# Both tiles' long products first, and their diagonal blocks behind them, at eleven of 32 places of a fused attention and mixture-of-experts kernel

## What is computed

```python
q = q * cos + _rotate_half(q) * sin
k = k * cos + _rotate_half(k) * sin
attn = jnp.einsum('bhqd,bhkd->bhqk', q, k) * SCALE
diff = jnp.where(diff > 0, 0.0, diff)          # pos[key] - pos[query]
attn = attn + (diff[None, :, :] * slopes[:, None, None] * MAX_BIAS)[None]
w = jax.nn.softmax(attn, axis=-1)
out = jnp.einsum('bhqk,bhkd->bhqd', w, v)
```

## Time and profile before

| | |
|---|---|
| median of 3 runs | 1626.6 us (1621.5 to 1634.37) |
| span of the profiled execution | 1580.1 us |
| own time of the profiled execution | not recorded apart; the median is 46.5 us above its span |
| TensorE busy | 1439.4 us, 91% |
| VectorE busy | 1180.2 us, 75% |
| ScalarE busy | 1020.6 us, 65% |
| GpSimd busy | 720.8 us, 46% |
| mean granted TensorE clock | 0.955 |
| first and last score product | 28.1 and 1380.4 us |

### The profile page before, as it was taken

One profiled execution on the slowest core, in us unless ns is written; L12 is line 12 of the kernel. 1 busy time (PEld: TensorE's weight loads), 2 busy tenths in 40 slices (PEclk: granted clock), 3 DMA queues, 4 the chain that ended last, 5 costly groups with the idle time before them and its releaser, 6 DMA issues.

```text
span 1580.1 us, 33006 instructions
## 1 busy us (share of the span) xinstructions
PE 1439.4 (91%) x11110; PEld 785.8 (50%) x11110; DVE 1180.2 (75%) x2631; ACT 1020.6 (65%) x1742; POOL 720.8 (46%) x655
## 2 busy tenths in 40 slices
PE   8988999999999989899999999998999899998937
PEld 4433444444444435455555544454455555664625
DVE  7675787888787897766776778877877677736875
ACT  1365766676767656777777676766677676776242
POOL 3233353736455434552534354543647443437550
PEclk8699999999999999999999999999999999999969
DMA  7435344333343424455545434354577576697451
GB/s 208 131 93 177 101 132 118 118 104 120 112 138 113 127 87 134 160 169 155 184 152 167 158 113 129 111 159 135 173 233 227 182 228 205 215 290 223 139 167 41
DMA packets 176390, 242.00 MB, mean 153 GB/s; under 512 B 58024, under 2 KB 94975, under 8 KB 176223
## 3 DMA queue, kind: packets, MB, share of 16 engines
q1 hardware_dynamic: 145786, 181.18, 38.0%
q0 software_dynamic: 10752, 29.37, 5.9%
q10 hardware_dynamic: 19684, 29.33, 5.4%
HBM read 152.53 MB, written 91.44 MB: 154 GB/s over the span
## 4 chain that ended last, share of the span: by engine, by line
PE 60%; DVE 17%; DMA 6%; SPq 5%; issue 5%; POOL 4%; ACT 2%; ACTq 0%; POOLq 0%; DVEq 0%
PE pS L660 17%; PE pV L702 11%; PE pG L726 6%; DVE negm L951 6%; PE pG L735 4%; PE pG L829 3%; PE pG L837 3%; PE pG L748 3%; PE pS L666 3%; PE pG L821 2%; DMA d_rec<-scr 1%; POOL d_x L1611 1%; PE pG L797 1%; SPq L503 1%; PE pG L851 1%
## 5 line engine op out<-in xcount | busy, mean ns | idle before, releaser
L951 DVE TENSOR_REDUCE negm<-pS 128x1 f32<-128x512 f32 x1024 | 657.9, 682 | 261.8 <-PE pS L666 256.6
L1389 ACT ACTIVATE ee<-pT,slp 128x512 f32<-128x512 f32 x1024 | 648.8, 684 | 224.0 <-PE pT L687 222.0
L660 PE MATMUL pS<-ka,qa 62*128 62x512 f32 x1024 | 477.1, 502 | 72.1 <-DVE negm L951 63.7
L681 PE MATMUL pT<-qa,ka 64*128 64x512 f32 x1024 | 472.0, 496 | 0.2 <-ACT ee L1389 0.2
L660 PEld LDWEIGHTS pS<-ka,qa 62*128 62x128 f32 x1024 | 195.6, 191 | 337.9 <-issue 323.6
L702 PE MATMUL pV<-ee,vv 128*32 128x512 f32 (+1 forms) x2048 | 284.0, 627 | 0.0
L666 PE MATMUL pS<-mAB,tri 64*128 64x64 bf16 x2048 | 241.5, 199 | 0.0
L687 PE MATMUL pT<-mAB,tri 64*128 64x64 bf16 x2048 | 237.6, 197 | 0.0
L1576 POOL TENSOR_TENSOR raw<-raw,rope 128x512 f32<-128x512 f32 x61 | 78.4, 1285 | 273.2 <-DVE sh L986 273.0
L681 PEld LDWEIGHTS pT<-qa,ka 64*128 64x128 f32 x1024 | 192.9, 188 | 3.9 <-issue 3.1
L666 PEld LDWEIGHTS pS<-mAB,tri 64*128 64x128 bf16 x2048 | 118.6, 98 | 139.4 <-issue 110.6
(11 more groups left out here) (198 smaller groups left out, 2181.2 us busy)
## 6 DMA issues: line engine op xcount, KB each, us to landing
d_part<-parts SPq DMA_DIRECT2D x63, 512.0 KB, 2.8
qa<-d_part SPq DMA_DIRECT2D x378, 64.0 KB
wb<-in_wb SPq DMA_DIRECT2D x77, 256.5 KB
xg<-d_x SPq DMA_DIRECT2D x77, 256.0 KB, 2.9
d_y<-yb ACTq DMA_DIRECT2D x77, 256.0 KB, 3.3
ka<-d_part SPq DMA_DIRECT2D x128, 128.0 KB
xT<-in_xT SPq DMA_DIRECT2D x16, 512.0 KB, 4.2
ka<-d_part SPq DMA_DIRECT2D x128, 64.0 KB
```

The lines of the kernel that those rows point to most:

```text
L660: e.matmul(pS[:, k, :], qa[g % 4][r, i, t * 128:t * 128 + 128].bitcast(F32R), ka[g % 4][r, i, :].bitcast(F32R), start=True, stop=False)
L681: e.matmul(pT[:, k, :], ka[g % 4][r, i, kt * 128:kt * 128 + 128].bitcast(F32R), qa[g % 4][r, i, :].bitcast(F32R), start=True, stop=False)
L951: e.tensor_reduce(negm[:, g % 2, j, t + k:t + k + 1], pS[:, k, :], AX, ALU.max, negate=True).then_inc(s_max, 1)
L1389: e.activation(ee[:, k, d % 7, :], pT[:, k, :], ACT.Exp, scale=slp[:, 6, h:h + 1]).then_inc(s_exp, 1)
```

## The change

A tuple names eleven places, and at these `pair(s)` no longer writes the blocks of tile 0 behind the long products of tile 0. It writes both long products of tile 0, both of tile 1, and then the blocks of tile 0 and of tile 1. At the other 21 places the order stays. No instruction is added or taken away, and the other engines' programs are the same.

```diff
 APART = tuple(range(32))
+LATE_BLOCKS = (0, 9, 10, 11, 22, 26, 27, 28, 29, 30, 31)
...
-            apart = s % 32 in APART
             for k in range(2):
                 if 0 <= s < NC:
                     score_rows(s, k)
                 if 0 <= d < NC:
                     turned_rows(d, k)
-                for kk in ((k,) if apart else (0, 1) if k == 1 else ()):
+                for kk in (() if s % 32 in LATE_BLOCKS and k == 0 else (0, 1) if s % 32 in LATE_BLOCKS else (k,)):
                     for a in range(2):
                         if 0 <= s < NC:
                             score_block(s, kk, a)
                         if 0 <= d < NC:
                             turned_block(d, kk, a)
```

## The result

The change made the kernel slightly slower in the comparison that belongs to the prediction: 1635.1 us (median of 20 runs) against 1629.9 us for the kernel before (20 runs in the same comparison), a ratio of 1.0044 with a 95% interval of 1.0024 to 1.0063. The medians lie 5.2 us apart, the ratio says some 7 us. The ratio leaves out one run of the kernel after, at 1652.3 us, that fell in a slow state. The forecast was 3.5 us less.

What follows compares the result with a forecast made beforehand. TensorE was taken as the bound in most steps, VectorE in some. Held places give back 0.43, clean places keep 0.65: -0.22 us a batch, -3.5 us in 16 batches, 1626.6 - 3.5 = 1623 us; range 1606 to 1637.

Steps and rivals of the forecast that it cites:

- The pair's saving, 0.13: At eleven late places the second long product's load hides under the first's columns, saving at most 0.13 us a pair.
- Rival 1: No load is hidden in the late pairs: a pair keeps its length, +0.45 us a batch, +7 us, 1634; chance 0.12.
- The sums' 0.21 us for 512 columns: Share of a long product's 0.34 us on TensorE; tile 0's second block starts at 0.34 + 0.21 + 0.05 = 0.60.
- The held and the clean places: Held: second long products wait for readers behind close late pairs, 0.43 us a batch given back; clean: five places keep 0.13.
- 10: Place 10, 2.05 us behind late place 9: second long product 0.11 late, net -0.02 us.
- 1 and 12 together: Old-order places behind late places 0 and 11: their second long products are held, +0.08 us together.
- 22: Late place 22 counted at nothing: the step behind it waits for VectorE, so nothing is lost or gained.
- "The median lies 46.5 us above that span and I leave this as it is.": Profiled span 1580.1 us against the median 1626.6; the gap was left unchanged and -3.5 us taken from the median.
- Rival 2: Readers on time at all eleven places, whole saving kept: 176 pairs x 0.13 = 23 us, 1604; chance 0.13.
- Rival 3: VectorE becomes the bound; late tiles' 0.21 and TensorE's 0.13 lost, at all 176 pairs +37 us, 1664; chance 0.11.
- all of 0.21: At late places tile 0's second block, and so VectorE's tile, comes 0.21 us later; rival 3 puts it all on the step.
- the sign by which rival 3 was to be known: L661's wait for `negm` grows from 63.7 us by 20 us or more, against little in the forecast.

Runs made afterwards that it cites:

- after_third: The kernel after, unchanged, run again in session 3 of the quick kind: ratio 0.9970 to the kernel before (1584.4 us).
- after_again: The kernel after, unchanged, run again in session 2 of the quick kind: ratio 0.9975 to the kernel before (1582.9 us).
- after_fourth: The kernel after, unchanged, run again in session 4 of the slower kind: ratio 1.0040 to the kernel before (1627.0 us).
- before_again: The kernel before, unchanged, traced once more in session 1: 1644.1 us, with a span of 1642.3 us.
- plain_after: The kernel after with GpSimd's indirect transfers made plain and expert blocks reading fixed rows, session 2: ratio 1.0080 to the kernel before.
- plain_before_3: The kernel before with GpSimd's indirect transfers made plain and expert blocks reading fixed rows, session 4: 1594.2 us, ratio 0.9776 to the kernel before.

## Why the prediction was wrong

**The pair's saving, 0.13.** Right in kind, too large: the load hides (0.11 behind the first), and a clean pair is 0.10 shorter. Rival 1 is out. The loads of the `fp32r` long products lie 0.11 apart. The load of the first `bf16` block comes later: 0.46 behind the second long product's load (455.68 less 455.22), and 0.23 behind the start of that product (455.45). By its record that product lasts until 455.84, so the trace doesn't show that the block's load waits for its end, as the prediction reads the earlier trace rows for rival 1.

The sums' 0.21 us for 512 columns, and with it the 0.13 that is left of 0.34, were the author's estimate; no run shows either. In their place the runs showed this: at place 26 the first block's load comes 0.57 behind the pair's first load (455.68 less 455.11), where two tiles' 0.34 are 0.68, so 0.11 is saved; and the second block of tile 0 starts 0.62 behind it (455.73), where the sums had 0.60 and place 27 before has 0.39, so 0.23 later and not 0.21.

The four of L829 in the earlier trace rows are the records of two products: L829 has 308 records for the 154 products of 77 blocks, while the `fp32r` L839 has 154 for 154 and L660 1024 for 1024. In that row the four start 0.215 to 0.216 us apart though each takes 0.38, so starts and not durations give the cost. The loads of the second, third and fourth start with the record ahead of their own (the second load and the first record both at 707.57) and take 0.19, less than the 0.215 from record to record, so they are hidden there.

**The held and the clean places.** Medians over the batches of the difference in a step's length, after_third less the first trace of before, both like the quick kind's, and what the forecast had:

| places | forecast | measured |
|---|---|---|
| 9, 11, 26, 30, 31 together | -0.65 | -0.49 |
| 27, 28, 29, 0 | +0.11, +0.07, +0.11, +0.08 | +0.09, +0.05, +0.08, +0.07 |
| 10 | -0.02 | -0.04 |
| 1 and 12 together | +0.08 | +0.03 |
| 22 | 0 | -0.03 |
| a batch | -0.22 | -0.24 |

Summed over all steps the two traces differ by -6.3 us, and after_again by -3.7; the spans differ by -3.3 and -0.7, since the tails are longer. The timed differences in the two sessions are -2 and -6 us in the medians, 0.25% and 0.30% by ratio. The sum of -3.5 us was right for the kind of session from which its trace came, its mechanism too. That it agrees this closely is partly luck: the clean places save 0.16 us a batch less than forecast, and the others give back 0.18 less.

**"The median lies 46.5 us above that span and I leave this as it is."** This is the step that failed. The 46.5 us were treated as a constant that the change can't touch, and so the term for what the change does to them was put at nothing. The runs showed that they are the distance between two kinds of session. The slower kind has tiles and other results of TensorE taken up late beside GpSimd's indirect transfers, of which the trace that was read has none, and there the same change is +0.44% and +0.40% (some 7 us), where it is -0.25% and -0.30% on the quick kind. The sentence behind it, that the change touches no other queue and only start times can shift, was true, and since nothing else differs in the programs, start times were enough. On the slower kind the order gains its 0.2 to 0.3 us a batch by the steps' medians as well (after_fourth less before_again: -0.31), which is 5 us in all, so it loses some 12 us elsewhere. What these 12 us are stays open. For the late starts speak that the sign goes with them (two sessions or comparisons of each kind), and that without indirect transfers both they and the distance between the kinds are gone. Against it stands that their sum in the kernel before (58.5 us) lies among those of the lists that lost (57.8 to 62.4). plain_after on the slower kind would decide and wasn't run there, and single traces scatter by as much as the effect.

**Rivals 2 and 3.** Rival 2 kept the whole saving; places 27, 28, 29 and 0 give it back. Rival 3 (VectorE the bound) did not come at eleven places: on the quick kind TensorE's wait for maxima is 67.3 us with the change against 63.7. At all 32 it came in part, +28 us of the 107 that all of 0.21 would be. That the wait was 82.2 us in the first trace of after, the sign by which rival 3 was to be known, was misleading: it is 76.0 us in before_again, without the change.

**The range.** 1606 to 1637 holds 1635.1, and within 1% was the class given the highest chance. The direction was wrong.

## What to carry to other kernels

Compare a trace's span with the median of its runs before anything is summed: a difference thirteen times the forecast effect is a part of the kernel that the trace doesn't show, and nothing says that the change leaves it alone. Before a reordering worth 0.3% is kept, time it in several sessions, since here it gained in two and lost in two. Where an engine's readers stand idle though the records of what they wait for have ended, look at what GpSimd issues at that time; and set their sum against what the stage is longer by, since much of such a wait can be made up for (in batches 1 to 13 of after, the late tiles are 26.5 us and the stage is 4.1 us longer).

## What the runs showed of the hardware

Every one of the 53 late tiles of after_fourth, and 50 of the 52 of before_again, lies within 1 us of an indirect transfer of GpSimd; such stretches are 26% of the span. In after_fourth 33 of the 53 are late while a tile of the other reader is, too, and TensorE is idle for more than 0.3 us beside 18 of them. In the record of semaphores, TensorE's signal for a tile at place 18 of batch 5 (the first trace of after) comes at 439.29, 1.99 us behind the end of the block's record at 437.30, and the next tile's follows after 0.10 us though their records lie 0.54 apart. So the signal, or TensorE's work behind its records, was held; which of the two can't be told, nor whether the kinds differ by the chip or by something else that lasts for a session. In plain_before_3 the plain transfers' records on GpSimd end before the data have landed: they take 0.55 us, and the scatters' data land 2.4 us after the issue. The indirect ones' records are longer, 1.00 us for the scatters and 0.95 for the gathers (after_fourth); whether GpSimd's longer work on them is what holds the others, no run here shows.

The kinds also differ on VectorE, the other way round: its sixteen `hs` (L1184) take 21.5 to 21.9 us in the five traces of the quick kind (the longest 3.1), and 10.1 to 17.9 in those of the slower one, 10.1 (the longest 0.68) in three of them. That isn't another price but another meeting. In all 15 traces with indirect transfers, the 164 records of `hs` with none of GpSimd's `TENSOR_TENSOR` beside them take 0.62 to 0.68 us, and all longer ones have one beside them: at 690.15 in the first trace of before `hs` takes 3.07 us beside one of 2.39 that starts at 690.27. In after_fourth an indirect transfer lies beside `hs` instead, `hs` is through in 0.63, and GpSimd's `TENSOR_TENSOR` starts 0.27 us behind its end. The quick kind is not quicker at everything.
